# A mixture-of-experts stage by units of one batch and one expert: accumulating DMAs against one-hot products

## The chip, the core and the metric

The kernel runs on one core of a Trainium2 chip. Its time is the device time of one execution in microseconds (us); the lowest is best. Three executions of the kernel before took 1070.01, 1071.24 and 1066.51 us, median 1070.01.

## The reference

Input x has 2 batches of 1024 tokens of 128 numbers. Four stages follow each other, each with a layer norm in front and its result added to x: attention a, feed-forward, attention b, and the same feed-forward again with the same weights. The change is in the feed-forward stage:

```python
capacity = max(1, int(Sz * CAP_FACTOR / E) + 1)          # 257 of 1024 tokens, 8 experts
scores = softmax(einsum('bsd,ed->bse', x, router_w))
gate_vals, sel_idx = top_k(swapaxes(scores, 1, 2), capacity)
tokens = x[b_idx, sel_idx]
h = gelu(einsum('becd,edh->bech', tokens, w1) + b1)      # 128 -> 512
y = einsum('bech,ehd->becd', h, w2) + b2                 # 512 -> 128
out = zeros_like(x).at[b_idx, sel_idx].add(y * gate_vals[..., None])
```

Each expert takes in each batch the 257 tokens that score highest for it. So a token can be taken by several experts or by none, and 257 is two full groups of 128 and one token more, the spare one.

## The kernel before, in words

Each stage is a block with a program for each engine; at the end of a block all engines meet. The feed-forward block (`feed_forward_stage`, L1174 on) first turns the normed tokens (`turn`, L1306), takes the router's logits, and finds each expert's threshold bit by bit in 30 steps (`step`, L1527). `number` and `columns` (L1552, L1561) then give each selected token its place, 1 to 257, in the list of its batch and expert. Meanwhile SyncE writes the normed tokens to a table in HBM (`scratch_xn`), with the 8 scores behind each row, and the residual x to another HBM buffer: `scratch_x` in the first feed-forward, the output itself in the second (`rows_out`, L1233). It also loads the matrices of all 8 experts.

What follows is a loop over 8 experts, both batches in one step:

- `one_hot` (L1577, VectorE) compares each token's place with 1 to 128, a tile of 128x2048 f16; `place_tokens` (L1321, TensorE) multiplies it with the tokens' numbers, which gives the list of rows to fetch, and `placing` (L1583) turns this into integers.
- `gather(e)` (L1258, GpSimd): five indirect DMAs, four of 128 rows (L1268) and one of the 2 spare rows (L1270), into one of 4 buffers `xg`.
- `turn_x` (L1331) transposes the rows into PSUM. `take_x` on ScalarE and `low_x` on VectorE write them as a high and a low fp32r part (`xr`).
- `hidden(e, j)` (L1345), j = 0 to 3: three products (high by high, high by low, low by high), each in two halves of 258 and 256 columns. ScalarE applies gelu to 128x514 (L1468) and makes the high part of two such tiles at once (L1474), VectorE the low part (`low`, L1594).
- `output(e)` (L1358): 24 products of the same widths, then `take_y` adds b2.
- `turn_y` (L1370) transposes back to tokens, `gate` (L1600, VectorE) multiplies with the scores into `yg`.
- `scatter(e)` (L1273, GpSimd): after the DMAs of the expert before have all landed, five indirect DMAs that add the rows to the HBM buffer of the residual (L1281 and L1283).

The order of the work is written out by hand. TensorE runs hidden(e), turn_y(e-2) behind hidden(e, 0), turn_x(e+1), output(e-1). GpSimd runs gather 0 to 3 and then, for each e, scatter(e) and gather(e+4):

```python
for e in range(XBUF):
    gather(e)
for e in range(NE):
    scatter(e)
    if e + XBUF < NE:
        gather(e + XBUF)
```

When all has been added, the first feed-forward loads x back from HBM in four DMAs (L1255), and the norm of attention b waits for them; in the second the last scatter ends the program. `keep_busy` (L378) issues products whose result nobody reads.

## Time and profile before

| what | value |
|---|---|
| three executions, median | 1070.01 us (1066.51 to 1071.24) |
| the profiled execution | 1074.57 us, of which its span is 1072.8 us |
| TensorE products / weight loads | 806.1 us (75%) / 498.0 us (46%) of the span |
| VectorE / ScalarE / GpSimd | 608.9 us (57%) / 470.8 us (44%) / 458.1 us (43%) |
| TensorE's granted clock over the span | 0.84 |
| expert loop with its lead-in, first feed-forward | from 391.5 us to 553.7 us |
| the same, second feed-forward | from 912.4 us to the end |

PE is TensorE, PEld its weight load, DVE VectorE, ACT ScalarE, POOL GpSimd, SP SyncE. A row of a timeline gives start and duration in us, engine, line, operation, the output and the inputs; rows of one kind that follow each other are merged, with their count behind x. The duration of a merged row of products runs to the modelled end of the last one. "idle before" is followed by what ended the idle time. A number at L is a line of the kernel before.

### The profile page before, as it was taken

How to read it: one execution, taken by the hardware profiler on the slowest of the kernel's cores; microseconds unless marked ns; L12 is line 12 of the kernel's file. 1: busy time of each engine (PE TensorE's matmuls, PEld its weight loads, DVE VectorE, ACT ScalarE, POOL GpSimd, SP SyncE). 2: the span in 40 equal slices, each digit the busy share in tenths (PEclk: the TensorE clock that was granted, in tenths of full speed). 3: DMA queues.
4: the chain of work that ended last, by engine and by line, in shares of the span. 5: the costliest groups of instructions: out<-in, count | busy, mean ns of one | idle time of the engine just before them, and what ended most of it. 6: DMA issues, size and time to landing. Idle time of an engine off the chain costs nothing. (4 is left out here: it accounts for less than half of the span.)

```text
span 1072.8 us, 14959 instructions
## 1 busy us (share of the span) xinstructions
PE 806.1 (75%) x5474; PEld 498.0 (46%) x5474; DVE 608.9 (57%) x1206; ACT 470.8 (44%) x892; POOL 458.1 (43%) x656
## 2 busy tenths in 40 slices
PE   3879999999988737565537999999998886374760
PEld 2545565566555316554424444444444352373650
DVE  4776677776734674422135767777776456562220
ACT  2325666666664005333204366666666610262330
POOL 1442454653331017888725113222232200688875
PEclk9989999999999556776859599999999975586785
DMA  3852343121113801122225260011000092112222
GB/s 89 239 140 51 122 120 89 50 71 60 60 42 96 299 6 37 24 30 31 27 50 147 67 170 19 14 32 31 2 2 2 1 316 79 29 23 31 34 28 20
DMA packets 58504, 74.56 MB, mean 69 GB/s; under 512 B 12848, under 2 KB 45312, under 8 KB 58048
## 3 DMA queue, kind: packets, MB, share of 16 engines
q1 hardware_dynamic: 36800, 60.11, 18.4%
q0 software_dynamic: 12288, 8.70, 6.3%
q10 hardware_dynamic: 9344, 4.80, 1.7%
q8 instruction: 44, 0.72, 0.3%
q14 instruction: 28, 0.23, 0.1%
HBM read 42.18 MB, written 30.29 MB: 68 GB/s over the span
## 5 line engine op out<-in xcount | busy, mean ns | idle before, releaser
L1029 ACT ACTIVATE b_pt<-b_banks 128x512 f32<-128x512 f32 (+1 forms) x320 | 154.8, 558 | 102.0 <-PE b_banks L943 101.8
L1052 DVE TENSOR_REDUCE a_mlate<-a_banks 128x2 f32<-128x1024 f32 (+3 forms) x120 | 124.8, 1080 | 50.3 <-PE a_banks L881 32.0
L1268 POOL DMA_INDIRECT f_xg<-scratch_xn,f_index x64 | 87.0, 1360 | 147.3 <-DVE f_index L1588 128.4
L1052 DVE TENSOR_REDUCE b_mlate<-b_banks 128x2 f32<-128x1024 f32 (+3 forms) x120 | 126.2, 1081 | 38.6 <-PE b_banks L891 19.5
L943 PE MATMUL a_banks<-a_q,a_k 121*128 121x512 f32 (+3 forms) x384 | 117.2, 383 | 4.8 <-DMA a_q<-a_mt 3.9
L1029 ACT ACTIVATE a_q_hl<-a_banks 128x512 f32<-128x512 f32 (+1 forms) x160 | 81.8, 557 | 66.9 <-PE a_banks L943 65.4
L881 PE MATMUL a_banks<-a_k,a_q 120*128 120x512 f32 (+3 forms) x384 | 99.0, 360 | 11.2 <-DVE a_mlate L1052 7.5
L943 PE MATMUL b_banks<-b_q,b_k 64*128 64x512 f32 (+3 forms) x384 | 99.6, 424 | 10.0 <-ACT b_pt L1029 8.7
L1029 ACT ACTIVATE a_k_hl<-a_banks 128x512 f32<-128x512 f32 (+1 forms) x160 | 82.2, 557 | 53.3 <-PE a_banks L943 51.8
L807 POOL TENSOR_SCALAR_AFFINE_SELECT b_pt<-b_pt 128x128 f32<-128x128 f32 x128 | 37.1, 295 | 136.5 <-ACT b_pt L1029 136.5
L943 PEld LDWEIGHTS a_banks<-a_q,a_k 121*128 121x128 f32 x384 | 65.1, 190 | 50.0 <-issue 20.2
L943 PEld LDWEIGHTS b_banks<-b_q,b_k 64*128 64x128 f32 x384 | 48.1, 191 | 85.5 <-ACT b_pt L1029 55.5
L1433 ACT ACTIVATE f_xr<-f_banks 128x514 fp32r<-128x514 f32 x16 | 9.5, 593 | 171.3 <-PE f_banks L1343 171.3
L881 PE MATMUL b_banks<-b_k,b_q 63*128 63x512 f32 (+3 forms) x384 | 77.8, 396 | 8.2 <-DVE b_mlate L1052 4.5
L961 PE MATMUL b_banks<-b_pt,vg 128*32 128x512 f32 (+3 forms) x768 | 81.7, 517 | 0.0
L881 PEld LDWEIGHTS a_banks<-a_k,a_q 120*128 120x128 f32 x384 | 64.1, 191 | 26.9 <-DVE a_mlate L1052 16.7
L1342 PE MATMUL f_banks<-ident,f_xg 128*128 128x128 f32 x64 | 14.8, 375 | 75.0 <-DMA f_xg<-scratch_xn,f_index 75.0
L1354 PE MATMUL f_banks<-f_xr,f_w1r 128*128 128x258 f32 (+1 forms) x384 | 63.7, 320 | 9.4 <-DVE f_xr L1592 8.8
L1366 PE MATMUL f_banks<-f_hr,f_w2r 128*128 128x258 f32 (+1 forms) x384 | 66.1, 345 | 0.0
L1281 POOL DMA_INDIRECT out<-f_yg,f_index x32 | 56.9, 1777 | 15.9 <-issue 8.5
L1366 PEld LDWEIGHTS f_banks<-f_hr,f_w2r 128*128 128x128 f32 x384 | 63.0, 252 | 0.2
L1354 PEld LDWEIGHTS f_banks<-f_xr,f_w1r 128*128 128x128 f32 x384 | 56.9, 221 | 12.6 <-issue 9.2
(227 smaller groups left out, 1389.8 us busy)
## 6 DMA issues: line engine op xcount, KB each, us to landing
scratch_w<-a_tab SPq DMA_DIRECT2D x16, 512.0 KB, 3.1
f_w1r<-scratch_w SPq DMA_DIRECT2D x16, 512.0 KB, 8.8
f_w2r<-scratch_w SPq DMA_DIRECT2D x16, 512.0 KB, 9.8
a_rot<-in_w SPq DMA_DIRECT2D x16, 256.0 KB, 4.0
a_q<-scratch_q SPq DMA_DIRECT2D x8, 384.0 KB
a_k<-scratch_k SPq DMA_DIRECT2D x8, 384.0 KB
scratch_q<-b_q_hl SPq DMA_DIRECT2D x24, 128.0 KB, 2.8
b_q<-scratch_q SPq DMA_DIRECT2D x32, 96.0 KB
```

The source lines that it names most:

```text
L807: pool.affine_select(out=block[:, 0:P], in_=block[:, 0:P], compare_op=ALU.is_ge, fill=0.0, base=0, pattern=[[1, P]], channel_multiplier=-1 ...
L881: last = pe.matmul(to[:, bank, col:col + w], head_rows(q2, n, h, slice(q * P, (q + 1) * P), 0), head_rows(k2, n, h, slice(k0, k0 + w), 0), ...
L943: last = pe.matmul(st[u % NST][:, col:col + w], head_rows(k2, n, h, slice(key * P, (key + 1) * P), 1), head_rows(q2, n, h, slice(c * CH + ...
L961: last = pe.matmul(o_ps[VW * h:VW * (h + 1), q0:CH], vg[n % 2][:, key, h, :], pt[(SET0[i] + s) % NPT][:, h, col:col + w], start=(key == 0) ...
L1029: act.activation(pt[at % NPT][:, h, 0:cols], st[u % NST][:, 0:cols], ACT.Exp, scale=scale).then_inc(exp_done, 1)
L1052: last = dve.tensor_reduce(dst, src, AX.X, ALU.max, negate=True)
L1268: pool.indirect_dma_start(to[:, i, :], None, m.scratch["xn"], bass.IndirectOffsetOnAxis(ap=index[:, e, at:at + 1], axis=0)).then_inc(xg_in ...
L1281: pool.indirect_dma_start(residual, bass.IndirectOffsetOnAxis(ap=index[:, e, at:at + 1], axis=0), of[:, i, :], None, compute_op=ALU.add).t ...
L1342: pe.transpose(xg_ps[:, PIECE[i]], of[:, i, 0:D], m.ident[:, :])
L1354: last = pe.matmul(h_ps[u % 2][:, half], w1r[e][:, wp, j * P:(j + 1) * P], xr[e % 2][xp][:, half], start=(i == 0), stop=(i == 2))
L1366: last = pe.matmul(y_ps[:, half], w2r[e][:, wp, j * P:(j + 1) * P], hr[e % 2][hp][:, j, half], start=(j == 0 and i == 0), stop=(j == HB - ...
L1433: act.activation(xr[e % 2][0][:, :], xg_ps, ACT.Copy).then_inc(x_high, 1)
```

## The change

The loop now runs over 16 units, batch 0 with its 8 experts and then batch 1 (`UNITS`). A unit has 256 tokens of one batch and expert. All 16 spare tokens are gathered once, by two indirect DMAs of 8 rows, and lie as two columns behind the 256 tokens of each expert in `xr`; so the products of a unit are 258 wide, and both batches' units of an expert compute both spare columns. A gather is two DMAs (L1297 of the changed kernel).

The outputs no longer go through HBM. `slots` (each token's place, by batch and expert) goes to HBM as f16, and SyncE loads the 1024 places of a unit's batch and expert into all 128 partitions (`spread_row`). VectorE compares them with the partition's own number: 128x2x1024, one-hot by token (`spot`). The gated output is split into a high part on ScalarE (`high_y`) and a low part on VectorE (`low_y`), and TensorE multiplies both with the one-hot rows and accumulates over the 8 experts of the batch in two PSUM banks (`scatter`, now TensorE's). At the end of a batch ScalarE copies the sum (`take_sum`), TensorE turns it (`turn_sum`), and VectorE adds it to x, which stays in SBUF (`finish`). The second feed-forward then stores x to the output in four DMAs; the first stores nothing, and attention b reads x where it is. The residual is no longer written out ahead of the loop. Twenty `keep_busy` products stand ahead of the first turn_x.

```diff
-SIDES = 2
-SLOTS = B * 256 + B
-FLAT = CH - 256 - B
+UNITS = B * NE
+SLOTS = 2 * P + B
 ROW = D + NE
-XBUF, AHEAD = 4, 3
-PER_EXPERT = 16 * (2 * B + 1)
...
     def vector(dve):
         link = chainer(dve, chain)
-        def measure(c):
-            if not latent:
-                dve.wait_ge(m.x_in[c], 16)
-            chunk_measure(dve, m, s, c)
-
         link(dve.tensor_copy(as_rows(wq[:, :]), by_row(m.w_q[:, :] if latent else m.w_qkv[:, 0:D])))
-        measure(0)
-        measure(1)
+        chunk_measure(dve, m, s, 0)
...
+    column = sb("column", [P, NT, NE], F16)
+    hot = [sb(f"hot_{i}", [P, NT // B, P], F16) for i in range(2)]
+    index, spare_index = sb("index", [P, UNITS, 2], I32), sb("spare_index", [NE, B], I32)
...
+    y = sb("y", [P, NE, SLOTS])
+    yg = [[sb(f"yg_{i}_{j}", [P, 2, D], F32R) for j in range(2)] for i in range(2)]
+    spare_y = [sb(f"spare_y_{j}", [NE, D], F32R) for j in range(2)]
+    spots = [sb(f"spots_{i}", [P, 2, T], F32R) for i in range(2)]
...
+    spread = [m.xt[:, i * T // 2:(i + 1) * T // 2].bitcast(F16) for i in range(2)]
...
+        def own_row(b):
+            if b:
+                sp.wait_ge(own_ready, past("own_ready", b))
+            sp.dma_start(own_slots[:, :], m.scratch["slots"][b]).then_inc(own_in, 16)
+
+        def spread_row(n):
+            b, e = divmod(n, NE)
+            if n >= 2:
+                sp.wait_ge(spots_ready, past("spots_ready", n - 1))
+            sp.dma_start(spread[n % 2], m.scratch["slots"][b, e:e + 1, :].to_broadcast([P, T])).then_inc(spread_in[n % 2], 16)
...
-        sp.wait_ge(added, past("added", PER_EXPERT * NE))
-        if not last_layer:
...
+        for n in range(2, UNITS):
+            spread_row(n)
+            if n == NE + 2:
+                own_row(1)
+        if last_layer:
+            stored = sem("stored")
             for c in range(NCH):
-                at = slice(c * TPC, (c + 1) * TPC)
-                sp.dma_start(m.x[:, at, :], residual.rearrange("(t p) d -> p t d", p=P)[:, at, :]).then_inc(m.x_in[c], 16)
+                sp.wait_ge(finished, past("finished", c + 1))
+                sp.dma_start(out.rearrange("b (t p) d -> p (b t) d", p=P)[:, c * TPC:(c + 1) * TPC, :],
+                             m.x[:, c * TPC:(c + 1) * TPC, :]).then_inc(stored, 16)
+            sp.wait_ge(stored, 16 * NCH)
...
-        def scatter(e):
-            pool.wait_ge(gated, past("gated", e + 1))
-            if e == 0:
-                pool.wait_ge(x_out, 16 * NCH)
-            else:
-                pool.wait_ge(added, past("added", PER_EXPERT * e))
-            of = yg[e % 2]
-            for i, at in enumerate(COLUMN):
-                pool.indirect_dma_start(residual, bass.IndirectOffsetOnAxis(ap=index[:, e, at:at + 1], axis=0), of[:, i, :], None,
-                                        compute_op=ALU.add).then_inc(added, 16)
-            pool.indirect_dma_start(residual, bass.IndirectOffsetOnAxis(ap=index[0:B, e, 2:3], axis=0),
...
+        def gather(n):
+            pool.wait_ge(placed, past("placed", n + 1))
+            if n >= XBUF // 2:
+                pool.wait_ge(xg_turned, past("xg_turned", n - XBUF // 2 + 1))
+            if n >= XBUF:
+                pool.wait_ge(y_low, past("y_low", n - XBUF + 1))
+            for i in range(2):
+                pool.indirect_dma_start(xg[n % XBUF][:, i, :], None, m.scratch["xn"],
+                                        bass.IndirectOffsetOnAxis(ap=index[:, n, i:i + 1], axis=0)
+                                        ).then_inc(xg_in[n % (XBUF // 2)], 16)
+
+        def gather_spares(b):
+            pool.wait_ge(spare_placed, past("spare_placed", 1))
+            pool.indirect_dma_start(spare_x[:, b, :], None, m.scratch["xn"],
+                                    bass.IndirectOffsetOnAxis(ap=spare_index[:, b:b + 1], axis=0)).then_inc(spare_in, 16)
+
+        pool.wait_ge(xn_out, past("xn_out", 16 * NCH))
+        pool.wait_ge(score_out, past("score_out", 16))
+        gather(0)
+        for b in range(B):
+            gather_spares(b)
+        for n in range(1, UNITS):
+            gather(n)
...
+        def turn_x(n):
+
+            pe.wait_ge(placed, past("placed", min(n + AHEAD - (n > 0), UNITS)))
+            pe.wait_ge(x_low, past("x_low", n))
+            if n == 1:
+                pe.wait_ge(spare_low, past("spare_low", 1))
+            if n and n + AHEAD - 1 < UNITS:
+                place_tokens(n + AHEAD - 1)
+            pe.wait_ge(xg_in[n % (XBUF // 2)], past("xg_in0", PER_UNIT * (n // (XBUF // 2) + 1)))
...
+        def turn_y(n):
+            b, e = divmod(n, NE)
+            pe.wait_ge(y_taken, past("y_taken", n + 1))
+            if n:
+                pe.wait_ge(y_low, past("y_low", n))
+            for i in range(2):
+                last = pe.transpose(yg_ps[:, i, :], y[:, e, i * P:(i + 1) * P], m.ident[:, :])
+            if e == NE - 1:
+                last = pe.transpose(spare_y_ps, y[:, :, 2 * P + b], m.ident[:, :])
+            last.then_inc(y_turned, 1)
+
+        def scatter(n):
+            b, e = divmod(n, NE)
+            pe.wait_ge(spots_ready, past("spots_ready", n + 1))
+            pe.wait_ge(y_low, past("y_low", n + 1))
+            if n == NE:
+                pe.wait_ge(sum_taken, past("sum_taken", B))
+            for c in range(NCH // B):
+                to = sum_ps[:, c, :]
+                for part in range(2):
+                    for i in range(2):
+                        last = pe.matmul(to, yg[n % 2][part][:, i, :], spots[n % 2][:, i, c * CH:(c + 1) * CH],
+                                         start=(e == 0 and part == 0 and i == 0), stop=False, skip_group_check=True)
+                if e == NE - 1:
+                    if c == 0:
+                        pe.wait_ge(own_ready, past("own_ready", b + 1))
+                    for part in range(2):
+                        last = pe.matmul(to, spare_y[part][:, :], own_spots[:, c * CH:(c + 1) * CH],
+                                         start=False, stop=(part == 1), skip_group_check=True)
+            last.then_inc(added, 1)
+
+        def turn_sum(c):
+            pe.wait_ge(sum_taken, past("sum_taken", c + 1))
+            if c in (1, 2):
+                pe.wait_ge(finished, past("finished", c))
+            for i in range(TPC):
+                at = (c % 2 * TPC + i) * P
+                last = pe.transpose(t_ps[c][:, i * P:(i + 1) * P], total_t[:, at:at + P], m.ident[:, :])
+            last.then_inc(sum_turned, 1)
...
+        place_spares()
+        for n in range(AHEAD):
+            if n:
+                pe.wait_ge(placed, past("placed", n))
+            place_tokens(n)
+        keep_busy(pe, m, banks[:, 5, 0:2 * P], IDLE["gather"])
         turn_x(0)
...
+        for n in range(UNITS):
+            hidden(n, 0)
+            hidden(n, 1)
+            if n >= 2:
+                turn_y(n - 2)
+            hidden(n, 2)
+            hidden(n, 3)
+            if n + 1 < UNITS:
+                turn_x(n + 1)
+            if n:
+                output(n - 1)
+            if n >= 2:
+                scatter(n - 2)
+            if n in (NE + 2, NE + 3):
+                turn_sum(n - NE - 2)
+        turn_y(UNITS - 2)
+        output(UNITS - 1)
+        scatter(UNITS - 2)
+        turn_y(UNITS - 1)
+        scatter(UNITS - 1)
+        turn_sum(2)
+        turn_sum(3)
 
...
+        def high_y(n):
+            b, e = divmod(n, NE)
+            act.wait_ge(y_turned, past("y_turned", n + 1))
+            if n >= 2:
+                act.wait_ge(added, past("added", n - 1))
+            if e == NE - 1:
+                act.wait_ge(spare_gated, past("spare_gated", 1))
+                act.activation(spare_y[0][:, :], spare_y_ps, ACT.Copy, scale=spare_gate[:, b:b + 1])
+            for i in range(2):
+                last = act.activation(yg[n % 2][0][:, i, :], yg_ps[:, i, :], ACT.Copy, scale=xg[n % XBUF][:, i, D + e:D + e + 1])
+            last.then_inc(y_high, 1)
+
+        def take_sum(c):
+            act.wait_ge(added, past("added", (c // 2 + 1) * NE))
+            act.activation(total_t[:, c % 2 * CH:(c % 2 + 1) * CH], sum_ps[:, c % 2, :], ACT.Copy).then_inc(sum_taken, 1)
 
         if projected:
...
+                if j == 1 and n >= 2:
+                    high_y(n - 2)
+            if n + 1 < UNITS:
+                take_x(n + 1)
+            if n:
+                take_y(n - 1)
+            if n == NE + 1:
+                take_sum(0)
+                take_sum(1)
+        high_y(UNITS - 2)
+        take_y(UNITS - 1)
+        high_y(UNITS - 1)
+        take_sum(2)
+        take_sum(3)
...
+        def one_hot(n):
+            b, e = divmod(n, NE)
+            if n >= 2:
+                dve.wait_ge(place_mm, past("place_mm", n - 1))
+            half = slice(b * NT // B, (b + 1) * NT // B)
+            dve.tensor_tensor(hot[n % 2][:, :, :], m.places[:, :].rearrange("p (o q) -> p o q", o=1).to_broadcast([P, NT // B, P]),
+                              column[:, half, e:e + 1].to_broadcast([P, NT // B, P]), ALU.is_equal).then_inc(hot_ready, 1)
...
+        def low(n, pair):
+            dve.wait_ge(h_high, past("h_high", 2 * n + pair + 1))
             at = slice(2 * pair, 2 * pair + 2)
-            dve.tensor_tensor(hr[e % 2][1][:, at, :], h[pair][:, :, :], hr[e % 2][0][:, at, :].bitcast(F32), ALU.subtract
+            dve.tensor_tensor(hr[n % 2][1][:, at, :], h[pair][:, :, :], hr[n % 2][0][:, at, :].bitcast(F32), ALU.subtract
                               ).then_inc(h_low, 1)
...
+        def low_y(n):
+            b, e = divmod(n, NE)
+            dve.wait_ge(y_high, past("y_high", n + 1))
+            if e == NE - 1:
+                dve.scalar_tensor_tensor(out=spare_y[1][:, :], in0=spare_y_ps, scalar=spare_gate[:, b:b + 1],
+                                         in1=spare_y[0][:, :].bitcast(F32), op0=ALU.mult, op1=ALU.subtract)
+            for i in range(2):
+                last = dve.scalar_tensor_tensor(out=yg[n % 2][1][:, i, :], in0=yg_ps[:, i, :], scalar=xg[n % XBUF][:, i, D + e:D + e + 1],
+                                                in1=yg[n % 2][0][:, i, :].bitcast(F32), op0=ALU.mult, op1=ALU.subtract)
+            last.then_inc(y_low, 1)
+
+        def spot(n):
+            dve.wait_ge(spread_in[n % 2], past("spread_in0", 16 * (n // 2 + 1)))
+            if n >= 2:
+                dve.wait_ge(added, past("added", n - 1))
+            for i in range(2):
+                last = dve.tensor_scalar(spots[n % 2][:, i, :], spread[n % 2], m.spot[:, i:i + 1], None, ALU.is_equal)
+            last.then_inc(spots_ready, 1)
...
+        def finish(c):
+            dve.wait_ge(sum_turned, past("sum_turned", c + 1))
+            dve.tensor_tensor(flat(m.x, c), flat(m.x, c), t_ps[c], ALU.add).then_inc(finished, 1)
...
+        spare_gates()
+        for n in range(UNITS):
+            if n >= 2:
+                low_y(n - 2)
+            low(n, 0)
+            if n + AHEAD + 1 < UNITS:
+                one_hot(n + AHEAD + 1)
+            low(n, 1)
+            if n + 1 < UNITS:
+                low_x(n + 1)
+            if n + AHEAD < UNITS:
+                placing(n + AHEAD)
+            if n in (2, NE + 4):
+                own_spot(n // NE)
+            if n:
+                spot(n)
+            if n in (NE + 2, NE + 3):
+                finish(n - NE - 2)
+        low_y(UNITS - 2)
+        low_y(UNITS - 1)
+        finish(2)
+        finish(3)
```

In the loop of TensorE, the changed kernel has in steady state, from the second half of the one-hot products (L1423; the same two rows stand ahead of them for the first 512 tokens) to the first output products (L1398):

```order
L1423 MATMUL f_banks<-f_spots,f_yg_0 128x512 x2
L1423 MATMUL f_banks<-f_spots,f_yg_1 128x512 x2
L1387 MATMUL f_banks<-f_xr,f_w1r 128x258 x6
L1408 MATMUL f_banks<-ident,f_y 128x128 x2
L1387 MATMUL f_banks<-f_xr,f_w1r 128x258 x6
L1347 MATMUL f_banks<-f_tokens,f_hot 128x2 x8
L1370 MATMUL f_banks<-ident,f_xg 128x128 x2
L1398 MATMUL f_banks<-f_hr_0,f_w2r 128x258
L1398 MATMUL f_banks<-f_hr_1,f_w2r 128x258
```

The eight products of 512 columns (L1423) are new; the 24 hidden and output products of a unit, the placing products and the transposes are half of what an expert had.

VectorE, one step of the loop before:

```order
L1606 TENSOR_TENSOR f_yg<-f_banks,f_xg 128x512
L1607 TENSOR_SCALAR f_yg<-f_banks,f_xg 2x128
L1580 TENSOR_TENSOR f_hot<-places,f_column_h 128x2048
L1597 TENSOR_TENSOR f_hr_1<-f_h,f_hr_0 128x1028 x2
L1592 TENSOR_TENSOR f_xr_1<-f_banks,f_xr_0 128x514
L1587 CAST f_index<-f_banks 128x6
L1588 ISA f_index<-f_index 2x2
```

and now (L1724 is low_y, L1714 low, L1680 one_hot, L1697 low_x, L1687 placing, L1733 spot):

```order
L1724 SCALAR_TENSOR_TENSOR f_yg_1<-f_banks,f_xg,f_yg_0 128x128 x2
L1714 TENSOR_TENSOR f_hr_1<-f_h,f_hr_0 128x516
L1680 TENSOR_TENSOR f_hot<-places,f_column 128x1024
L1714 TENSOR_TENSOR f_hr_1<-f_h,f_hr_0 128x516
L1697 TENSOR_TENSOR f_xr<-f_banks,f_xr 128x256
L1687 CAST f_index<-f_banks 128x2
L1733 TENSOR_SCALAR f_spots<-xt,spot 128x1024 x2
```

The one-hot tile stands between the two low parts, gating has become the low part of the gated output, and two comparisons of 1024 columns close the step.

## Rows read from the trace of the kernel before

**Rows 1.** Page: busy time by engine; granted TensorE clock in 40 slices, tenths.

```profile
PE 806.1 (75%) x5474; PEld 498.0 (46%) x5474; DVE 608.9 (57%) x1206; ACT 470.8 (44%) x892; POOL 458.1 (43%) x656
...
PEclk9989999999999556776859599999999975586785
```

**Rows 2.** Windows: length, busy (count) of PE, PEld, DVE, ACT, POOL; clock, DMA share, GB/s.

```profile
929.30:1066.00 136.70, 76.20 (x539) 69.66 (x539) 43.43 (x54) 47.23 (x64) 108.73 (x72) 0.72 0.24 29
1066.00:1072.80 6.80, 0.00 (x0) 0.00 (x0) 0.00 (x0) 0.00 (x0) 0.00 (x0) 0.50 0.01 0
```

**Rows 3.** Groups by line: scatter DMAs of the second feed-forward; TensorE transposing gathered rows.

```profile
L1281 POOL DMA_INDIRECT out<-f_yg,f_index x32 | 56.9, 1777 | 15.9 <-issue 8.5 <-DMA out<-f_yg,f_index 5.9 <-DVE f_yg L1607 1.5
...
L1342 PE MATMUL f_banks<-ident,f_xg 128*128 128x128 f32 x64 | 14.8, 375 | 75.0 <-DMA f_xg<-scratch_xn,f_index 75.0
```

**Rows 4.** Chain of waits: last scatter DMA of two experts that follow each other (start, us).

```profile
998.53 1.35 POOL out L1283
...
1015.30 1.34 POOL out L1283
```

**Rows 5.** Timeline, TensorE: hidden and output products of one expert.

```profile
1032.98 2.74 PE L1354 MATMUL f_banks<-f_xr,f_w1r 128*128 128x258 f32 x18
1035.56 3.02 PE L1366 MATMUL f_banks<-f_hr,f_w2r 128*128 128x258 f32 x24
```

**Rows 6.** Window: TensorE clock around the products of Rows 5.

```profile
1032.00:1042.00 10.00, 9.10 (x74) 8.42 (x73) 4.33 (x6) 5.76 (x8) 6.90 (x5) 1.00 0.31 27
```

**Rows 7.** Timeline, TensorE in attention a: products of 512 fp32r columns.

```profile
251.49 0.63 PE L943 MATMUL a_banks<-a_q,a_k 121*128 121x512 f32 x2
251.95 0.63 PE L881 MATMUL a_banks<-a_k,a_q 120*128 120x512 f32 x2
```

**Rows 8.** Timeline, TensorE: the first hidden products; and window: the clock there.

```profile
929.30 2.91 PE L1354 MATMUL f_banks<-f_xr,f_w1r 128*128 128x258 f32 x12 [1.51 <-DVE f_xr L1592]
...
929.30:933.00 3.70, 3.70 (x17) 3.70 (x18) 2.05 (x1) 1.84 (x4) 3.28 (x2) 0.50 0.15 33
```

**Rows 9.** Groups by shape, ScalarE: gelu; high part; scale and bias by pointer.

```profile
L1468 ACT ACTIVATE f_h<-f_banks,b_t 128x514 f32<-128x514 f32 x64 | 42.4, 684 | 22.5 <-PE f_banks L1354 22.2
L1474 ACT ACTIVATE f_hr<-f_h 128x1028 fp32r<-128x1028 f32 x32 | 34.0, 1062 | 1.0
...
L327 ACT ACTIVATE xn<-x,sc 128x128 f32<-128x128 f32 x32 | 13.1, 482 | 7.3 <-DVE sc L319 7.3
```

**Rows 10.** Groups by shape, VectorE: one-hot, low x, two operands of 128, cast.

```profile
L1580 DVE TENSOR_TENSOR f_hot<-places,f_column_h 128x2048 f16<-128x2048 f16 x16 | 36.3, 2277 | 0.1
...
L1592 DVE TENSOR_TENSOR f_xr<-f_banks,f_xr 128x514 fp32r<-128x514 f32 x16 | 11.1, 692 | 70.8 <-ACT f_xr L1433 70.8
...
L1571 DVE SCALAR_TENSOR_TENSOR f_tokens<-f_banks,tokens 128x128 f16<-128x128 f32 x6 | 1.6, 364 | 0.1
...
L1106 DVE CAST a_k<-a_k 96x1024 fp32r<-96x1024 f32 x1 | 0.7, 689 | 1.0 <-DMA a_k<-a_q 1.0
```

**Rows 11.** Timeline: a GpSimd gather DMA beside VectorE work; then one without.

```profile
460.73 4.47 POOL L1268 DMA_INDIRECT f_xg<-scratch_xn,f_index  x1 [0.30 <-issue]
...
460.87 2.27 DVE L1580 TENSOR_TENSOR f_hot<-places,f_column_h 128x2048 f16<-128x2048 f16 x1
...
463.07 1.21 DVE L1597 TENSOR_TENSOR f_hr<-f_h,f_hr 128x1028 fp32r<-128x1028 f32 x1
...
920.63 0.97 POOL L1268 DMA_INDIRECT f_xg<-scratch_xn,f_index  x1 [0.31 <-issue]
```

**Rows 12.** Timeline: lead-in of the loop, to the first transposes.

```profile
917.47 2.86 POOL L1268 DMA_INDIRECT f_xg<-scratch_xn,f_index  x1 [64.03 <-DVE f_index L1588]
...
926.51 1.08 PE L1342 MATMUL f_banks<-ident,f_xg 128*128 128x128 f32 x4 [6.23 <-DMA f_xg<-scratch_xn,f_index]
```

**Rows 13.** Timeline: the first VectorE instruction behind the first feed-forward.

```profile
553.71 0.28 DVE L459 COPY b_wq<-w_qkv 128x128 f32<-128x128 f32 x1 [26.28 <-PEq L1648]
```

**Rows 14.** DMAs that load x back (L1255): landing.

```profile
DMA to landing us min/median/max: 2.8/3.7/4.1
```

360 lines of the change are left out of this document (160 added, 200 removed).

## The prediction

> **What bounds the kernel now.** I read the page first [rows 1]: TensorE is busy 75% of the span, but its clock, at 0.9 to full through the first attention, falls to 0.5 to 0.8 in both feed-forwards. The windows say why [rows 2]: in the 136.7 us from the second feed-forward's first hidden product to its last scatter, GpSimd is busy 108.7 us and TensorE 76.2, at a mean clock of 0.72. A scatter DMA costs GpSimd 1.78 us in the mean, and over both loops TensorE sits idle 75.0 us ahead of the transposes of gathered rows, for the gather DMAs [rows 3]. In the chain of waits two experts' last scatters stand 16.8 us apart [rows 4]. So the bound is GpSimd's queue, in which each gather stands behind a scatter, and each scatter behind the landing of the one before. The end is a queue of scatters too: from the last GpSimd row to the end of the span nothing runs for 6.8 us [rows 2].
>
> **What TensorE needs.** At full clock [rows 6] 18 hidden products of an expert take 2.58 us to the start of the output products, with small waits for gelu, and the 24 output products 3.02 us [rows 5]: 0.125 us a product of 256 or 258 columns. A product of 512 fp32r columns takes 0.23: two of L943 start at 251.49, the next at 251.95 [rows 7]. A unit of the changed kernel has 24 products of 258 (3.0 us), 8 scatter products of 512 (1.9), 8 placing products (0.3) and 4 transposes (0.6): 5.8 us, sixteen times. The scatter products are all the new work there, 30 us a layer. That fits under the 16.8 us that an expert, two units, now takes only if nothing else of a unit takes longer.
>
> **What the other engines need.** ScalarE, from [rows 9]: gelu 0.684 at 514 columns, so about 0.45 at 258; the high part 1.06 at 1028, so 0.6 at 516; the two gated high parts at the 0.41 that each of 32 tiles with pointers takes (13.1 / 32). With take_x 0.35 and take_y 0.45 a unit is 1.8 + 1.2 + 0.8 + 0.8 = 4.6 us. VectorE, from [rows 10]: one_hot 1.15 (half of 2.28), two low parts of 516 at 0.69, low_x 0.4, low_y 2 x 0.3, placing 0.15, and the two comparisons of 1024. For those no row exists. The cast of 1024 columns from f32 to fp32r took 0.69; the subtraction of two operands takes 1.21 for 1028 [rows 11]. I take 0.69, since a comparison with one tensor operand is nearest to the cast; this makes 5.1 us a unit, and 6.1 at the other bound. Both stay off the path: the comparisons stand last in VectorE's step and start when TensorE has finished scatter(n-2) at the end of unit n; after them VectorE still waits for the high part of y. The DVE perf modes page of the Trainium skill (VectorE: DVE Perf Modes, section Mode 2x_2P) says that a `tensor_scalar` between two SBUF tiles runs at two elements a cycle even in fp32; by it the comparison is 0.69 rather than 1.21, and only VectorE's slack would change.
>
> **The chain inside a unit.** No engine is full, so I add the path that repeats: hidden(n,0) 0.5 to its result; gelu, gelu, high part 0.45 + 0.45 + 0.6; high_y(n-2) 0.8; then on VectorE low_y 0.6, low 0.69, one_hot 1.15, low 0.69, low_x(n+1) 0.4; then hidden(n+1,0). That is 6.35 us, and six handovers between engines at about 0.05 make 6.6. The one_hot stands inside this path. What queues behind ScalarE's new wait for turn_y(n-2) is gelu(n,2), and behind VectorE's wait for y_high are both low parts and low_x; that is how the new step sets the period. I put 0.2 on top for stretches at the lower clock, since TensorE is busy only 5.8 of 6.6 us: **6.8 us a unit**, where before two units took 16.8.
>
> **Lead-in.** Columns take 0.6 us less (two operations fewer, one cast more). Two one-hot tiles of half the width save 2.3 us before the first index. GpSimd issues 2 + 2 DMAs instead of 5 ahead of the first transposes, but the 2 spare ones are waited for by turn_x(0), so that saves one, 1.3 us with its gap. Against that stand the spares' placing, their copies and splits, and spot(0) ahead of low_x(0), 1.2 us together. Instead of at 929.3 [rows 8] I expect the first hidden product at 926.3. The keep_busy products fill the wait of 6.2 us for the gather [rows 12] and cost nothing; without that wait they would cost 4 us.
>
> **Seam and tail.** Where batch 0 ends, ScalarE copies two banks (1.2), VectorE builds own_spot and finishes two chunks (2.1), partly in its slack: 2.5 us. The sixteenth unit then ends at 926.3 + 16 x 6.8 + 2.5 = 1037.6. Behind it: output(15) 1.5, scatter(14) 1.9, turn_y(15), high_y and low_y with the spare 2.8, twelve scatter products 2.8, two copies 1.2, four transposes 0.6, finish 0.7, and 2.0 because parts of this will run at 1.2 GHz: 13.5 us to the last finish, 1051.1. The store needs an HBM landing, 2.8 to 4.1 us for the DMAs of x [rows 14], and the last landing is followed by some 4 us before the span ends (6.8 less a scatter's landing of about 2.5): 1059.1 instead of 1072.8, **13.7 us** gained.
>
> **First feed-forward.** Its loop runs 520.9 us earlier than the second one's, so its last finish is at 530.2. Attention b began at 553.7 [rows 13], after all scatters, their landing and the reload; now x is already in SBUF and the block has only to end, for which I take 1 us: 531.2, **22.5 us** gained. The residual stores are gone; they lay beside other work and save nothing. The loads of the experts' matrices are as before and stay hidden.
>
> **Sum.** 13.7 + 22.5 = 36.2 us: 1038.4 for the profiled execution, which was 1074.6 and so 4.6 above the median of the runs. Against the median 1070.0 the forecast is **1034**. Each 0.1 us of a unit is 3.2 us of the whole; the gain is gone at 7.93 us a unit.
>
> **The rivals.**
> - *TensorE-bound.* If VectorE's and ScalarE's operations overlap better than I added them, the period is TensorE's 5.8: 1034 - 32 = 1002. For it: merged rows show operations starting before the last one ends. Against it: the path above has no slack that I can name. 0.12.
> - *One stretch at half clock in every unit.* The window around [rows 5] holds the full clock with TensorE busy 9.10 of 10 us; here it is busy 5.8 of 6.6, with two pauses. If a third of the work runs at 1.2 GHz, TensorE needs about 7.5: 1034 + 0.7 x 32 = 1056. 0.14.
> - *The low clock stays* (the slower one). At 0.50, twelve products took 2.91 us [rows 8], 0.23 to 0.24 each; a unit is then 5.6 + 3.5 + 0.9 = 10 us and the kernel 1034 + 3.2 x 32 = 1136. It decides from more than about half of the products at 1.2 GHz. Against it: at 1.2 GHz TensorE would have no pause left, and the page has the clock at 0.6 to 0.8 in slices 36 to 39 although TensorE idled more than it will now [rows 1]. 0.08.
> - *GpSimd and VectorE lock each other.* The gather DMA at 460.73 took 4.47 us beside 3.48 us of VectorE work with SBUF operands, one without took 0.97 [rows 11]; so GpSimd stood still for VectorE. A unit now has 3.9 us of such work (one_hot, two lows, two comparisons) and two gathers of 0.97 + 0.31: 6.5 us, just under the period. If VectorE has to wait for GpSimd likewise, its path grows by 1.9: 8.5 us a unit, 1034 + 1.7 x 32 = 1088. In the rows one_hot shows no such waiting: 16 of them average 2.277. The page SBUF — State Buffer (on the shared port pair) states that whichever of the two starts first holds the pair for its whole instruction and the other fully blocks; the trace agrees for GpSimd's side alone. By this rule read both ways the time would be that 1088. 0.03.
> - *The gathers stay late*, and the change does not do what it says: with GpSimd's 6.5 us a unit and a DMA's landing uneven, TensorE would wait some units for rows. With 1 us a unit for this, 1034 + 32 = 1066; 0.03.
>
> **How the numbers follow.** My forecast has the remaining 0.60. About 0.5%, 5 us, is what a measurement of this kernel tells from no change. Faster by more than that: 0.60 + 0.12 and nearly all of the half-clock case, 0.85; within it 0.04, late gathers above all; slower 0.08 + 0.03 = 0.11. The range leaves out the two rivals above 1064 and most of the TensorE-bound case: 1004 (5.85 us a unit) to 1064 (7.75).
>
> **What would show it.** In the profile after: hidden(n,0) of neighbouring units 6.6 to 7.0 us apart; the comparisons at 0.7 each; no idle time ahead of the gathered rows' transposes (L1370) beyond the lead-in; GpSimd below half busy in the loop; a clock above 0.9 there; the first norm of attention b near 531. A wrong period with idle TensorE ahead of hidden for low_x says that the path was mis-added; idle time for the gather DMAs says GpSimd; a clock near 0.6 says the third rival. A spread row that lands late would show as VectorE waiting for a DMA ahead of L1733.

## The result and the profile after

| what | before | changed kernel |
|---|---|---|
| median of the runs | 1068.26 us (1066.42 to 1071.24) | 998.1 us (995.38 to 1001.5) |
| ratio, 95% interval | | 0.934 (0.930 to 0.939) |
| profiled execution, its span | 1074.57, 1072.8 us | 995.38, 993.6 us |
| forecast of the median | | 1034 us, range 1004 to 1064 |

The direction was right. The gain is 70 us where 36 were forecast, and the time lies 6 us below the range: the forecast was wrong. The changed kernel was run once more beside an experiment and gave 997.42 us (992.86 to 1001.41).

From the page of the changed kernel, busy time of TensorE and its granted clock in 40 slices, against [rows 1]:

```profile
PE 861.4 (87%) x5826; PEld 531.6 (54%) x5826; DVE 666.3 (67%) x1390; ACT 510.9 (51%) x1098; POOL 295.1 (30%) x566
...
PEclk9998999999999955799979699999999997569998
```

TensorE is busy 87% of the span, not 75%, and inside both feed-forward loops (slices 18 to 20 and 37 to 39) its digit is 9 and the clock's 9 as well. The windows say the same (length, then busy time and count of PE, PEld, DVE, ACT, POOL; clock, DMA share, GB/s); the first row is the loop of the first feed-forward, the others the loop and the tail of the second:

```profile
410.00:500.00 90.00, 87.87 (x643) 75.35 (x642) 68.61 (x131) 60.12 (x150) 28.06 (x24) 0.99 0.23 59
880.00:935.00 55.00, 51.48 (x372) 43.73 (x372) 40.58 (x77) 35.67 (x87) 20.48 (x19) 0.92 0.24 57
935.00:978.00 43.00, 42.51 (x303) 36.73 (x301) 31.24 (x62) 29.23 (x75) 10.18 (x10) 1.00 0.26 67
978.00:990.00 12.00, 8.96 (x31) 5.67 (x31) 1.82 (x6) 2.36 (x6) 0.00 (x0) 0.79 0.00 1
```

In [rows 2] GpSimd was busy 80% of the loop at a TensorE clock of 0.72. Now it is busy 24 to 37%, and TensorE 94 to 99% at 0.92 to 1.00. In groups by line and shape (count, busy us, mean ns, idle time before them and what ended it), against [rows 3, 11]:

```profile
L1297 POOL DMA_INDIRECT f_xg<-scratch_xn,f_index x64 | 72.0, 1125 | 227.8 <-DVE f_index L1687 216.8 <-issue 11.0
L1733 DVE TENSOR_SCALAR f_spots<-xt,spot 128x1024 fp32r<-128x1024 f16 x64 | 45.2, 748 | 7.5 <-PE f_banks L1423 5.2 <-PE f_banks L1429 2.2
L1387 PE MATMUL f_banks<-f_xr,f_w1r 128*128 128x258 f32 x384 | 67.2, 315 | 10.3 <-DVE f_xr L1697 9.6 <-ACT f_h L1561 0.8
...
L1370 PE MATMUL f_banks<-ident,f_xg 128*128 128x128 f32 x64 | 14.2, 306 | 0.5 <-DMA f_xg<-scratch_xn,f_index 0.5
```

The 75.0 us in which TensorE idled ahead of gathered rows are 0.5 (L1370). A comparison of `spot` lasts 0.75 us (0.73 to 0.78 in all 64), and two that follow each other 1.42 us together, near the 0.69 that was chosen and far from the other bound of 1.21. The Trainium skill (VectorE: DVE Perf Modes, Mode 2×_2P) says that a `tensor_scalar` between two SBUF tiles runs at two elements a cycle even in fp32. The trace agrees: `one_hot`, which compares two tensors over the same 1024 columns, takes 1.21 us.

Where the gain lies, from first and last rows of each stage in the two profiled executions:

| stretch | before | after | gain | forecast |
|---|---|---|---|---|
| start to the first feed-forward's memset | 335.32 | 333.41 | 1.9 | 0 |
| first feed-forward, to attention b's first row on VectorE | 218.39 | 180.12 | 38.3 | 22.5 |
| attention b, to the second feed-forward's memset | 305.92 | 304.37 | 1.6 | 0 |
| second feed-forward, to the end of the span | 213.17 | 175.70 | 37.5 | 13.7 |

So the gain lies in the feed-forwards, as forecast. It is their size that is off. The two profiled executions lie 79.2 us apart and the medians 70.2, because the one before was 6.3 us above its median and the one after 2.7 below; so the gains of this table are together 9 us too large for the medians, and what each stage has of the 9 is not known.

**One unit.** The distance between two `low_y` on VectorE is the period. In the second feed-forward six follow each other at 6.12 us; then come 6.62 and 7.40 at the seam (where batch 0 ends), 6.14 and 6.13, then 5.69, 5.44 and 5.44 in units that build no one-hot tile any more, and 4.3 and 4.4 in the tail. The first feed-forward has the same figures within 0.03 us. Ahead of these, the first two units take 5.76 us each: they have no outputs to place yet. From one unit, TensorE's timeline (start and duration in us):

```profile
907.33 2.02 PE L1423 MATMUL f_banks<-f_spots,f_yg 128*128 128x512 f32 x8
909.53 0.95 PE L1387 MATMUL f_banks<-f_xr,f_w1r 128*128 128x258 f32 x6 [0.17 <-DVE f_xr L1697]
910.32 0.39 PE L1408 MATMUL f_banks<-ident,f_y 128*128 128x128 f32 x2
910.69 0.99 PE L1387 MATMUL f_banks<-f_xr,f_w1r 128*128 128x258 f32 x6
...
911.91 1.68 PE L1398 MATMUL f_banks<-f_hr,f_w2r 128*128 128x258 f32 x12
```

ScalarE's:

```profile
910.16 0.84 ACT L1561 ACTIVATE f_h<-f_banks,b_t 128x258 f32<-128x258 f32 x2 [2.06 <-PE f_banks L1387]
911.03 0.64 ACT L1567 ACTIVATE f_hr<-f_h 128x516 fp32r<-128x516 f32 x1
911.57 0.60 ACT L1526 ACTIVATE f_yg<-f_banks,f_xg 128x128 fp32r<-128x128 f32 x2
```

VectorE's:

```profile
912.21 0.61 DVE L1724 SCALAR_TENSOR_TENSOR f_yg<-f_banks,f_xg,f_yg 128x128 fp32r<-128x128 f32 x2 [1.33 <-ACT f_yg L1526]
912.74 0.69 DVE L1714 TENSOR_TENSOR f_hr<-f_h,f_hr 128x516 fp32r<-128x516 f32 x1
913.34 1.22 DVE L1680 TENSOR_TENSOR f_hot<-places,f_column 128x1024 f16<-128x1024 f16 x1
914.48 0.69 DVE L1714 TENSOR_TENSOR f_hr<-f_h,f_hr 128x516 fp32r<-128x516 f32 x1
915.08 0.42 DVE L1697 TENSOR_TENSOR f_xr<-f_banks,f_xr 128x256 fp32r<-128x256 f32 x1
```

This is the chain that the prediction added. The steps from start to start: hidden to gelu 0.63, gelus 0.87, high part 0.54, `high_y` 0.64, `low_y` 0.53, `low` 0.60, `one_hot` 1.14, `low` 0.60, `low_x` to the next hidden products (915.64) 0.56. That makes 6.11 us. TensorE waits 0.17 to 0.20 us for `low_x`, once a unit.

### The profile page after: what moved, and what is told of

Same layout as the page of the kernel before. It is cut to its first block and busy times, and to the rows that moved or that the text cites. A ratio compares the mean times of both kernels' runs of the same rounds, so it can differ in the third digit from the quotient of the medians.

```text
span 993.6 us, 16204 instructions
## 1 busy us (share of the span) xinstructions
PE 861.4 (87%) x5826; PEld 531.6 (54%) x5826; DVE 666.3 (67%) x1390; ACT 510.9 (51%) x1098; POOL 295.1 (30%) x566
## 5 line engine op out<-in xcount | busy, mean ns | idle before, releaser
L1297 POOL DMA_INDIRECT f_xg<-scratch_xn,f_index x64 | 72.0, 1125 | 227.8 <-DVE f_index L1687 216.8
L879 PE MATMUL b_banks<-b_k,b_q 63*128 63x512 f32 (+3 forms) x384 | 75.5, 383 | 9.9 <-DVE b_mlate L1050 6.2
L1561 ACT ACTIVATE f_h<-f_banks,b_t 128x258 f32<-128x258 f32 x128 | 54.7, 476 | 53.0 <-PE f_banks L1387 51.4
L1387 PE MATMUL f_banks<-f_xr,f_w1r 128*128 128x258 f32 x384 | 67.2, 315 | 10.3 <-DVE f_xr L1697 9.6
L1423 PE MATMUL f_banks<-f_spots,f_yg 128*128 128x512 f32 x256 | 67.3, 403 | 4.9 <-DVE f_yg L1724 4.9
L385 PE MATMUL f_banks<-mask_s,ident_b 128*128 128x256 bf16 x294 | 66.5, 372 | 1.0 <-PEq L1144 1.0
L1050 DVE TENSOR_REDUCE b_mearly<-b_banks 128x2 f32<-128x768 f32 (+3 forms) x56 | 49.7, 917 | 22.9 <-PE b_banks L889 22.2
L1050 DVE TENSOR_REDUCE a_mearly<-a_banks 128x2 f32<-128x768 f32 (+3 forms) x56 | 49.6, 916 | 20.1 <-PE a_banks L889 19.1
```

Of the source, the lines that this page charges most:

```text
L385: pe.matmul(to.rearrange("p (a w) -> p a w", a=2), m.ident_b[:, :], m.mask_s[:, :, :], start=True, stop=True, skip_group_check=True)
L879: last = pe.matmul(to[:, bank, col:col + w], head_rows(q2, n, h, slice(q * P, (q + 1) * P), 0), head_rows(k2, n, h, slice(k0, k0 + w), 0), ...
L1050: last = dve.tensor_reduce(dst, src, AX.X, ALU.max, negate=True)
L1297: pool.indirect_dma_start(xg[n % XBUF][:, i, :], None, m.scratch["xn"], bass.IndirectOffsetOnAxis(ap=index[:, n, i:i + 1], axis=0)).then_i ...
L1387: last = pe.matmul(h_ps[u % 2], w1r[e][:, wp, j * P:(j + 1) * P], xr[xp][:, e, :], start=(i == 0), stop=(i == 2))
L1423: last = pe.matmul(to, yg[n % 2][part][:, i, :], spots[n % 2][:, i, c * CH:(c + 1) * CH], start=(e == 0 and part == 0 and i == 0), stop=Fa ...
```

## The experiments

Two theories were set against each other. *Path*: the chain above, with one_hot in it, sets 6.12 us. *TensorE*: its products set the period, and the one-hot products are a third of their time (1.85 us from their first start to the next hidden product's, in a unit of 5.68). Beside each time stands the length of the second feed-forward's loop, from the first `low_y` (L1724) to the last, which is 88.16 us in the changed kernel. This length repeats within 0.1 us between the two feed-forwards and between runs. The rest does not: the changed kernel itself took from 992.9 to 1001.5 us in its executions, and the stretch from the last `low_y` of the first feed-forward to the first one of the second 386.1 to 391.0 us in the three kernels that only reorder the loop, where two traces of the changed kernel have 388.3 and 389.6. So a difference of 3 us between two medians needs the loop's length beside it.

| kernel | median us (lowest to highest) | ratio to before (95%) | loop, us |
|---|---|---|---|
| changed kernel | 998.1 (995.4 to 1001.5) | 0.934 (0.930 to 0.939) | 88.16 |
| one_hot behind placing | 987.59 (986.5 to 991.6) | 0.924 (0.921 to 0.927) | 85.1 |
| low part ahead of low_y | 988.37 (986.1 to 992.1) | 0.926 (0.922 to 0.930) | 85.10 |
| both moves | 991.75 (990.2 to 996.7) | 0.929 (0.924 to 0.933) | 85.04 |
| one_hot twice | 1019.87 (1017.4 to 1022.4) | 0.953 (0.950 to 0.956) | 98.47 |
| 2 of 8 one-hot products | 980.03 (979.4 to 983.0) | 0.917 (0.914 to 0.919) | 83.83 |
| one_hot late and 2 of 8 products | 969.06 (968.3 to 969.9) | 0.900 (0.895 to 0.905) | 76.15 |
| no keep_busy ahead of turn_x | 999.06 (998.3 to 1001.6) | 0.935 (0.931 to 0.939) | 88.25 |
| late gather | 1003.67 (1000.5 to 1005.4) | 0.938 (0.934 to 0.942) | 88.24 |
| before, without scatter DMAs | 947.15 (941.5 to 955.4) | 0.883 (0.880 to 0.887) | - |

### one_hot behind placing

```diff
             low(n, 0)
-            if n + AHEAD + 1 < UNITS:
-                one_hot(n + AHEAD + 1)
             low(n, 1)
...
                 placing(n + AHEAD)
+            if n + AHEAD + 1 < UNITS:
+                one_hot(n + AHEAD + 1)
```

> The changed kernel's profile has the steady unit at 6.12 us with TensorE waiting for low_x, and 5.45 us in the last units, which have no one_hot and no placing products. Theory (path): the unit is set by the path hidden, gelu, high part, high_y, low_y, low, one_hot, low, low_x. With one_hot behind placing, off this path, it falls by 1.14 to 4.98, below TensorE's 5.45 plus 0.3 for placing, so the unit becomes 5.75: 12 units of 16 in each layer gain 0.37, about 9 us in all, 989 us. Rival (TensorE full): the unit is TensorE's own work with its gaps, and nothing changes, 998 us.

Measured 987.59 us, 10.5 less. In batch 0 the units stand 5.68 us apart instead of 6.12. The window of 34 us in that stretch:

```profile
895.00:929.00 34.00, 34.00 (x267) 30.30 (x266) 28.67 (x55) 23.90 (x61) 16.96 (x14) 1.00 0.28 74
```

VectorE there, at its second low part:

```profile
907.96 0.70 DVE L1714 TENSOR_TENSOR f_hr<-f_h,f_hr 128x516 fp32r<-128x516 f32 x1 [0.19 <-ACT f_hr L1567]
908.57 0.42 DVE L1697 TENSOR_TENSOR f_xr<-f_banks,f_xr 128x256 fp32r<-128x256 f32 x1
...
908.98 1.21 DVE L1680 TENSOR_TENSOR f_hot<-places,f_column 128x1024 f16<-128x1024 f16 x1
```

TensorE has no pause left, and VectorE now waits 0.2 us for ScalarE's second high part: the path that is left runs through ScalarE (its length is measured below, with two of eight products). One_hot on the path is shown to cost 0.44 us a unit, not its 1.14, since at 5.68 TensorE takes over. In the first two whole units of batch 1 the period stays at 6.12 even so. TensorE's rows tell why (L1439 turns the sum of batch 0, between the one-hot products and the next hidden ones):

```profile
938.42 1.99 PE L1423 MATMUL f_banks<-f_spots,f_yg 128*128 128x512 f32 x8
940.25 0.60 PE L1439 MATMUL f_banks<-ident,v 128*128 128x128 f32 x4
940.60 0.97 PE L1387 MATMUL f_banks<-f_xr,f_w1r 128*128 128x258 f32 x6
```

Four more transposes stand there, 0.35 us to the next start. Added to 5.68 they make 6.03; the last 0.09 to 6.12 is not explained. That TensorE's products decide there too is seen below: with two of eight of them these two units take 5.47 and 5.27 us. The loops give 3.1 us each, 6.2 of the 10.5; the rest lies outside them, where executions differ by as much.

### The low part ahead of low_y, and both moves

```diff
         for n in range(UNITS):
+            low(n, 0)
             if n >= 2:
                 low_y(n - 2)
-            low(n, 0)
```

> Only low(n,0) ahead of low_y(n-2); one_hot stays in the path. Theory (path): low(n,0), 0.60 us, runs while ScalarE makes high_y, so the unit falls from 6.12 to TensorE's 5.75 or a little below the path's 5.52: 9 us less, 989 us. Rival (TensorE full): no change, 998 us.

The kernel with both moves has this edit and that of "one_hot behind placing" together.

> One_hot behind placing, and low(n,0) ahead of low_y(n-2), so that VectorE makes the first low part while ScalarE makes the gated high part. Theory (path): the path falls below TensorE's 5.75 us with one_hot late alone, so low_y's move adds nothing beyond it where TensorE is full: 987 to 989 us. Rival (the path still decides with one_hot late): 0.5 us more in 28 units, about 975 us.

Measured 988.37 us, and 991.75 with both moves. The first takes the first low part (0.60) out of the path, since VectorE now makes it while ScalarE makes `high_y`; one_hot stays in the path, and the loop is 85.10 us. Its window of 34 us has TensorE without a pause, as with one_hot behind placing:

```profile
893.00:927.00 34.00, 34.00 (x267) 30.25 (x266) 28.53 (x55) 23.94 (x61) 12.86 (x12) 1.00 0.26 72
```

With both moves the loop is 85.04. So whichever of the two is taken from the path, the loop ends at the same length: the next limit is not on VectorE. The 991.75 us of both moves is no loss by the second move: the loops are equal, and the time is lost outside.

### one_hot twice

```diff
+    again = sb("again", [P, NT // B, P], F16)
...
+            if n > AHEAD:
+                dve.tensor_tensor(again[:, :, :], m.places[:, :].rearrange(...), ..., ALU.is_equal)
             dve.tensor_tensor(hot[n % 2][:, :, :], ...
```

> In front of each of 12 one_hot instructions a layer the same comparison is made once more into a tile that nobody reads. Theory (path): 1.14 us more in 24 units, 1025 us. Rival (TensorE full): VectorE is idle 1.4 us in each unit and takes it there, under 5 us more.

Measured 1019.87 us, 22 more; the loop grew by 10.3 us. Units went from 6.12 to 7.26, by one_hot's own 1.14, wherever one_hot was on the path: nine times between the first and the last `low_y`, which is the 10.3. At the seam (7.40, now 7.39) it was not, and in the last units there is none. The rival's "below 1003" is out.

### Two of eight one-hot products

```diff
-                for part in range(2):
-                    for i in range(2):
+                for part in range(1, 2):
+                    for i in range(1, 2):
...
-                                         start=(e == 0 and part == 0 and i == 0), stop=False, skip_group_check=True)
+                                         start=(e == 0), stop=False, skip_group_check=True)
```

> Leaves out three of four one-hot products of 512 columns (the high parts, and the first 128 tokens of the low part), so the output is only a quarter of the sum; the two products that stay keep the order of the waits. Theory (path): the loop keeps its 6.12 us, only the last units (5.45 to about 5.0) and the tail (12 products to 6) gain, about 4 us a layer, 990 us. Rival (TensorE full): 6 x 0.21 us less in each of 32 units, 40 us less, 958 us.

Measured 980.03 us, 18 less: more than the path theory said, less than half of TensorE's. The steady period is 6.12 as before, with 1.4 us of products gone from each unit. Only where TensorE was the limit did time go: the seam (7.40 to 6.10), the last units (5.69 to 5.28, and 5.44 to 5.27) and the tail (4.3 and 4.4 to 3.3 and 3.0), 4.3 us a layer, and 2.5 more behind each loop, to the last `finish`. The expectation had 4 us a layer for the last units and the tail, and nothing for the seam. The window of 36 us, with TensorE busy 78% and the period unchanged:

```profile
885.00:921.00 36.00, 27.91 (x224) 23.79 (x224) 28.42 (x55) 23.34 (x59) 13.81 (x12) 0.95 0.23 57
```

### one_hot late and two of eight products

The edits of "one_hot behind placing" and of "two of eight one-hot products" together.

> The kernel with one_hot behind placing, and with 2 of the 8 one-hot products of 512 columns per unit instead of 8 (a token then gets a quarter of its expert outputs). It asks what ends a unit once one_hot is off the path, where units stand 5.68 us apart. If that is TensorE, which was busy in all of the 34 us looked at, taking 6 x 0.23 = 1.4 us of products out must shorten a unit until the next limit: 5.68 to about 5.3, the distance of those units in the kernel with few products that have no one_hot in them (5.28). Twelve such units a layer, the seam and the tails as in the kernel with few products alone: the time is then about 980 less 24 x 0.8 = 961 to 972. Rival: ScalarE's and VectorE's path through a unit is the limit at 5.68, the products are hidden, and the time is some 978 to 980, from tails alone.

Measured 969.06 us, and the loop fell from 85.1 to 76.15 us, 9 us, where the same products were worth 4.3 with one_hot in its place. The steady units stand 5.27 us apart.

```profile
880.00:900.00 20.00, 17.01 (x140) 14.36 (x138) 18.48 (x37) 14.94 (x39) 11.71 (x8) 1.00 0.28 81
```

TensorE is down to 85% busy. So at 5.68 the products were the limit. At 5.27 it is a path again (TensorE waits 0.74 us for `low_x`), but another one than in the changed kernel: from `high_y` it goes on in ScalarE, over the second pair of gelus and the second high part, for which VectorE waits 0.20 us:

```profile
888.21 0.96 PE L1387 MATMUL f_banks<-f_xr,f_w1r 128*128 128x258 f32 x6 [0.74 <-DVE f_xr L1697]
...
891.64 0.64 ACT L1567 ACTIVATE f_hr<-f_h 128x516 fp32r<-128x516 f32 x1
...
892.31 0.70 DVE L1714 TENSOR_TENSOR f_hr<-f_h,f_hr 128x516 fp32r<-128x516 f32 x1 [0.20 <-ACT f_hr L1567]
```

From start to start: hidden to gelu 0.64, gelus 0.87, high part 0.54, `high_y` 0.50, gelus 0.88, high part 0.67, `low` 0.61, `low_x` to the next hidden products 0.57, together 5.28 us.

### The scatter DMAs left out of the kernel before

```diff
-            for i, at in enumerate(COLUMN):
-                pool.indirect_dma_start(residual, ..., of[:, i, :], None, compute_op=ALU.add).then_inc(added, 16)
-            pool.indirect_dma_start(residual, ..., of[0:B, 2 * B, :], None, compute_op=ALU.add).then_inc(added, 16)
+            pool.nop().then_inc(added, PER_EXPERT)
```

> The kernel before without its scatter DMAs: the output lacks both feed-forwards' sums, all else is computed. Theory (GpSimd's queue): one expert falls from 16.8 to about 10 us, which TensorE and the one-hot tile need, and no scatter stands behind the last product: about 50 us less a layer, 970 us. Rival (what holds the loop is the gathers' own latency and the low clock, not the scatters in front of them): under 30 us less in all beyond the two tails of 25 us, so about 1000 us.

Measured 947.15 us, 123 less. From its chain of waits (start, us):

```profile
894.63 2.21 DVE f_hot L1576
898.17 3.07 PE f_banks L1362 x24
901.24 0.72 PE f_banks L1350 x6
903.76 2.21 DVE f_hot L1576
...
912.90 2.21 DVE f_hot L1576
```

An expert, both batches, takes 9.13 us (894.63, 903.76, 912.90) where it took 16.8 [rows 4], and one_hot stands in the path there too. The window of two experts:

```profile
894.63:912.90 18.27, 16.39 (x150) 14.79 (x150) 12.64 (x17) 11.68 (x17) 14.46 (x10) 1.00 0.12 28
```

So where experts follow each other steadily, 7.7 us of each were the scatter DMAs. Not every expert is such: in the kernel before, the first four of the second feed-forward begin their hidden products 8.9 to 9.3 us apart, and only then come 23.1, 18.0, 16.9 and 16.9; here all eight stand 8.3 to 9.3 us apart. A measure of the whole is the time from the first hidden product of the second feed-forward to the end of the span: 143.5 us before, 80.1 without the scatter DMAs (in the slowest of its executions, 955.42 us), 114.0 in the changed kernel. The change gets back 29.5 of these 63.4 us. What the other 33.9 pay for no run separates; the largest new work are the one-hot products, 16 x 1.85 = 30 us of TensorE by an estimate from the rows above.

### A late gather

```diff
+        pool.wait_ge(sum_taken, past("sum_taken", NCH))
+        late = sem("late")
+        pool.indirect_dma_start(xg[0][:, 0, :], None, m.scratch["xn"],
+                                bass.IndirectOffsetOnAxis(ap=index[:, 0, 0:1], axis=0)).then_inc(late, 16)
+        pool.wait_ge(late, 16)
```

> One more gather DMA of 128 rows on GpSimd, issued in each layer after the last sum has been copied; its rows are not read. In the changed kernel the first instruction of attention b starts 0.3 us after the last finish, and the span ends 2.8 us after it; before, it took 3.3 us and more from the last DMA issue of a layer. Theory (a block that ends with a DMA of GpSimd pays for closing its queue): the end of each layer comes 3 us or more after that DMA has landed, 6 to 9 us more in all. Rival (only the landing counts): the first layer ends at most 2 us later, the second not at all, under 3 us more.

Measured 1003.67 us, 5.6 more, between the two. The rows at the end of its first feed-forward, and at the end of the program:

```profile
513.01 0.94 POOL L1315 DMA_INDIRECT f_xg<-scratch_xn,f_index  x1 [27.57 <-ACT v L1536]
...
514.32 0.69 DVE L1749 TENSOR_TENSOR x<-x,f_banks 128x512 f32<-128x512 f32 x1 [0.17 <-PE f_banks L1444]
...
518.94 0.28 DVE L457 COPY b_wq<-w_qkv 128x128 f32<-128x128 f32 x1 [3.93 <-PEq L1801]
```

```profile
997.66 0.94 POOL L1315 DMA_INDIRECT f_xg<-scratch_xn,f_index  x1 [27.85 <-ACT v L1536]
...
998.97 0.69 DVE L1749 TENSOR_TENSOR x<-x,f_banks 128x512 f32<-128x512 f32 x1 [0.16 <-PE f_banks L1444]
```

From the last finish to attention b's first row there are now 3.9 us instead of 0.3. The gather lands 2.5 us after its start, at 515.5, and the next block begins 3.4 us later. At the program's end it lands at 1000.2, 3.3 us before the span ends. The last store would hold the end until about 1002.7 in any case (3.0 us to landing, the median of its line), so there are only 3.8 instead of 2.8 us from the last finish to the end. Together 4.6 us. So here a block that ends on GpSimd's DMA pays over 3 us behind its landing; one that ends on VectorE pays 0.3, and in the changed kernel the span ends at about the landing of SyncE's last store. Why it is so, the traces do not show.

### No keep_busy products ahead of turn_x

```diff
-IDLE = {... "gather": 20, ...}
+IDLE = {... "gather": 0, ...}
```

> The 20 keep_busy products ahead of turn_x(0) are left out. Theory: the first 12 hidden products already run at the low clock with them (3.2 us for 12), so they help little; without them the clock rises one stretch later at most: 0 to 3 us more in all, 998 to 1001 us. Rival (they are what keeps the loop's clock at 0.99): the clock in the loop falls and the time rises by 10 us or more.

Measured 999.06 us, 1 us more than the changed kernel and inside its spread, with the same loop. They cost nothing and bring nothing that this can show.

## Why the prediction was wrong

**The bound** was named rightly: without the scatter DMAs the kernel before takes 123 us less, and in the changed kernel TensorE no longer waits for gathered rows. The 16.8 us, though, are not what every expert took (see that experiment); the sum does not use them.

**The chain inside a unit** is the step that failed: "6.35 us, and six handovers between engines at about 0.05 make 6.6 ... I put 0.2 on top". The links are the right ones, and the 6.8 us measured 6.12. The terms as listed add up to 6.33 (the prediction has 6.35) and measured 6.11 from start to start; what was put on top of them, 0.3 for handovers and 0.2 for the clock, is not in the rows. The durations of rows already contain the handover: an operation starts about 0.09 us before the row ahead of it ends (913.34 + 1.22 is 914.56, the next starts at 914.48), so steps have to be added from start to start. And the clock was full from the third unit to the last. This is 0.68 us for each unit, 22 us of the 36 that the median missed (43 by the two traces). The prediction also gave all 16 units the same length: the last four have no one_hot, the first two nothing to place, and the seam took 1.8 us instead of 2.5. Together this is worth another 4 us a layer. From the first hidden product to the end of the sixteenth unit it took 96.4 us and not 111.3.

**What TensorE needs** was right: 5.8 forecast, 5.68 measured once one_hot was off the path. The rival *TensorE-bound* gave a time (1002) nearer to the result than the forecast did, but that is luck: its mechanism decides only at the seam, in the last units and in the tail.

**Lead-in.** 3.0 us forecast; from the transpose of the places to the first hidden product it took 13.92 instead of 20.47 us, and the part ahead of that was 1.4 shorter. Its rows in the changed kernel:

```profile
865.72 0.48 PE L1466 MATMUL f_banks<-ident,f_slots 128*128 128x128 f32 x1 [0.90 <-DVE f_slots_h L1662]
...
868.15 1.22 DVE L1680 TENSOR_TENSOR f_hot<-places,f_column 128x1024 f16<-128x1024 f16 x1
...
871.44 1.20 POOL L1297 DMA_INDIRECT f_xg<-scratch_xn,f_index  x1 [59.56 <-DVE f_index L1687]
...
875.46 0.87 POOL L1303 DMA_INDIRECT f_spare_x<-scratch_xn,f_spare_index  x1 [0.30 <-issue]
...
876.03 0.38 PE L1370 MATMUL f_banks<-ident,f_xg 128*128 128x128 f32 x2
...
878.11 0.29 PE L1374 MATMUL f_banks<-ident,f_spare_x 8*128 8x8 f32 x2 [1.70 <-DMA f_spare_x<-scratch_xn,f_spare_index]
...
879.64 3.21 PE L1387 MATMUL f_banks<-f_xr,f_w1r 128*128 128x258 f32 x12 [1.25 <-DVE f_xr L1697]
```

Columns gave 1.2 us (0.6 forecast), the first one-hot tile 1.8 (2.3 forecast). From the first gather to the end of the last one that turn_x(0) needs it is 4.9 instead of 7.9 us: one DMA less, as forecast, and the first gather takes 1.20 instead of 2.86 [rows 12], which was not. The 1.2 us charged against it for the spare rows and spot(0) lay beside the wait for the gather. TensorE still waited 1.70 us there for the spare rows (L1374).

**Tail.** 14.7 us instead of 13.5 to the last finish; the clock there was 0.79, more of it low than the 2.0 us allowed for.

**The end** is the second step that failed: "the last landing is followed by some 4 us before the span ends". That belongs to GpSimd's DMAs. (It was also read too short: the last scatter DMA starts at 1064.61, its line lands 2.6 us after the start in the median, and so some 5.6 us were left before the end, by this estimate.) Here the last finish is followed by 2.8 us, store included, where 8.0 were forecast:

```profile
989.94 1.23 SPq L1285 DMA_DIRECT2D out<-x  x2
990.08 0.69 DVE L1744 TENSOR_TENSOR x<-x,f_banks 128x512 f32<-128x512 f32 x1 [0.17 <-PE f_banks L1439]
```

Between the feed-forward and attention b 1 us was allowed; it is 0.3 (513.53 - 513.22):

```profile
512.53 0.69 DVE L1744 TENSOR_TENSOR x<-x,f_banks 128x512 f32<-128x512 f32 x1 [0.17 <-PE f_banks L1439]
...
513.53 0.28 DVE L457 COPY b_wq<-w_qkv 128x128 f32<-128x128 f32 x1 [0.32 <-PEq L1796]
```

**The first feed-forward** was taken at the second one's gain and so repeats its errors. By them it should have gained 41.8; it gained 38.3, mostly because its first hidden products came 3.2 us later against the second one's than before. The traces place this: VectorE's wait for the router's logits grew from 4.82 to 6.26 us in the first feed-forward and fell from 6.18 to 4.51 in the second. Its cause is open.

**The other rivals.** The half clock was in the first two units alone: 0.50 from 879.64 to 885.40 us and 0.66 to 891.16, where twelve hidden products take 3.21 us; from there to 978 us it is 1.00. Those two units were the shortest of their loop up to the seam all the same, 5.76 us. GpSimd was slowed, its gathers 1.13 us in the mean against 0.97 alone, and VectorE was not: one_hot took 1.20 to 1.22 in every unit, so the runs show the lock only in the direction of [rows 11]. The Trainium skill (SBUF — State Buffer, on the shared port pair) has it work both ways; nothing here shows VectorE's side. The clock stayed at 0.95 to 1.00 even with TensorE busy 78 to 85% (the two kernels with few products).

## What to carry to other kernels

Add a chain from start to start of neighbouring rows, not from durations plus handovers, and write beside it how many of the loop's steps really hold each link. When the queue that bounds a loop is taken away, compute the two next limits apart (here the path, 6.12, and TensorE, 5.68): the distance between them is what an order of the same instructions can still give, and moving one_hot or one low part gave it, 987.6 and 988.4 us, better than both kernels. Move one and measure the loop before moving the second: behind the next limit it brings nothing.
